# Values of two attention units multiplied in one block, and a new order of the split work in the projections

## The reference, cut to what matters

```python
h = _layernorm(x, axis=-1) * (1 + ca) + sa
Q = X @ W_q.T;  K = X @ W_k.T;  V = X @ W_v.T          # 16 heads of 16 features
Qr = _rope(Qh, cos, sin);  Kr = _rope(Kh, cos, sin)
scores = jnp.einsum('bhqd,bhkd->bhqk', Qr, Kr) * DH ** (-0.5)
scores = jnp.where(causal[None, None], neg, scores)
pattern = jax.nn.softmax(scores, axis=-1)
heads = jnp.einsum('bhqk,bhkd->bhqd', pattern, Vh)
```

## Time and profile before

| | |
|---|---|
| median of 3 runs | 2427.26 us (2424.31 to 2429.4) |
| profiled execution, its time | 2421.51 us |
| profiled execution, its span | 2419.7 us |
| PE busy over the span | 2186.0 us (90%) |
| DVE busy | 1670.5 us (69%) |
| ACT busy | 1299.3 us (54%) |
| mean granted PE clock | 0.949 of full |
| projections, from the span's start to the first products of attention | some 176 us |
| the stages of attention | 215.1 to about 1082 us |
| everything behind attention | some 1338 us |

### The profile page before, as it was taken

The page is one execution under the profiler, slowest core; times in us unless marked ns, Lnnn a source line. Parts: engine busy times, 40 slices in busy tenths (PEclk is TensorE's granted clock), DMA queues, the critical chain, the costliest instruction groups (busy, mean ns, idle before and its releaser), DMA issues. The chain is left out here.

```text
span 2419.7 us, 38970 instructions
## 1 busy us (share of the span) xinstructions
PE 2186.0 (90%) x12976; PEld 1396.1 (58%) x12976; DVE 1670.5 (69%) x2718; ACT 1299.3 (54%) x2506; POOL 878.8 (36%) x1060
## 2 busy tenths in 40 slices
PE   7878999999999999988999599963999999999991
PEld 6752333333333333326777456643888898888891
DVE  7758787878778787815777778874555655555566
ACT  4533777777677777773332344421555555555553
POOL 4552330313121220212555422454345444445351
PEclk9986999999999999999999899985999999999996
DMA  5669025436161611003000100113544434444426
GB/s 199 147 161 124 1 77 110 84 86 115 55 130 57 124 72 46 1 16 121 1 0 0 34 1 1 36 44 125 182 146 142 145 136 140 162 170 142 138 75 222
DMA packets 127399, 227.92 MB, mean 94 GB/s; under 512 B 16689, under 2 KB 91057, under 8 KB 126833
## 3 DMA queue, kind: packets, MB, share of 16 engines
q1 hardware_dynamic: 112672, 180.95, 22.2%
q0 software_dynamic: 14544, 44.61, 11.0%
HBM read 146.65 MB, written 78.48 MB: 93 GB/s over the span
## 5 line engine op out<-in xcount | busy, mean ns | idle before, releaser
L232 DVE TENSOR_REDUCE tile_max<-p_m 128x2 f32<-128x1024 f32 (+1 forms) x628 | 641.9, 1065 | 133.8 <-PE p_m L224 66.7
L1021 ACT ACTIVATE probs<-p_s 128x512 f32<-128x512 f32 (+3 forms) x1280 | 596.4, 534 | 238.5 <-PE p_s L924 233.3
L2302 PE MATMUL p_up<-f_xT,f_w 128*128 128x512 f32 (+1 forms) x2304 | 464.5, 351 | 12.8 <-issue 5.9
L2302 PEld LDWEIGHTS p_up<-f_xT,f_w 128*128 128x128 f32 x2304 | 368.3, 189 | 66.4 <-issue 16.3
L864 POOL TENSOR_SCALAR_AFFINE_SELECT probs<-probs 128x128 f32<-128x128 f32 x512 | 145.3, 293 | 694.0 <-ACT probs L1021 685.2
L221 PE MATMUL p_m<-ka,qa 96*128 96x512 bf16 (+1 forms) x1256 | 352.3, 363 | 12.7 <-DVE tile_max L232 5.0
L924 PE MATMUL p_s<-qa,ka 99*128 99x512 bf16 (+3 forms) x1280 | 351.3, 351 | 13.1 <-ACT probs L1021 7.1
L2471 POOL TENSOR_TENSOR f_w<-f_raw,f_w 128x1024 fp32r<-128x1024 f32 x95 | 231.8, 2450 | 357.1 <-ACT f_w L2357 357.1
L938 PE MATMUL p_o<-probs,va 128*32 128x512 f32 (+3 forms) x2560 | 300.2, 541 | 0.8 <-issue 0.5
L2317 PE MATMUL p_y<-f_w,f_hidden 128*128 128x256 f32 x1872 | 251.1, 280 | 1.0 <-DVE f_hidden L2424 0.6
L221 PEld LDWEIGHTS p_m<-ka,qa 96*128 96x128 bf16 x1256 | 108.3, 99 | 237.7 <-DVE tile_max L232 135.7
(11 more groups left out here) (285 smaller groups left out, 2640.1 us busy)
## 6 DMA issues: line engine op xcount, KB each, us to landing
x_slots<-mods SPq DMA_DIRECT2D x73, 516.0 KB, 4.0
f_raw<-in_W SPq DMA_DIRECT2D x24, 1024.0 KB, 10.9
f_raw<-in_W1a SPq DMA_DIRECT2D x23, 1024.0 KB, 6.0
f_raw<-in_W1b SPq DMA_DIRECT2D x23, 1024.0 KB, 8.3
qk_scr<-parts SPq DMA_DIRECT2D x48, 256.0 KB, 2.8
qa<-qk_scr POOLq DMA_DIRECT2D x42, 256.0 KB, 15.6
ka<-qk_scr POOLq DMA_DIRECT2D x42, 256.0 KB, 17.4
g_ys<-y_rows SPq DMA_DIRECT2D x16, 512.0 KB, 8.8
```

The source lines that it names most:

```text
L232: return nc.vector.tensor_reduce(out=k.tile_max[:, 2 * hp:2 * hp + 2, i, bank], in_=products[:, :, 0:width], op=ALU.max, axis=AX.X)
L1021: nc.scalar.activation(probs[:, (buf * UNITS + n) % NPROBS, h, lo:CH], p_s[:, s_bank(("exp", HG * n + h), buf), lo:CH], ACT.Exp, scale=DH ...
L2302: last = nc.tensor.matmul(p_up[:, f % 2, ab, 0:size], w1[:, wh, ab * KT + kt, f * P:(f + 1) * P], xT[:, t % 2, xh, kt, 0:size], start=(kt, ...
```

## The change

In attention, the values of units n-2 and n-1 are multiplied together at the end of every even unit n, behind both groups of products for the maxima. The buffers for probabilities grow from three to four. In the projections ACT centers the next chunk first and rounds the next chunk's `hT` behind the first part of Q; DVE subtracts Q's first part before it takes K's first half, and makes the rest of `hT` behind that.

```diff
@@ projections, DVE
+                    split(i, 0)
+                    rotate(i, 1, range(1))
                     rest_of_hT(i + 1, 1 - par)
-                    rotate(i, 1, range(1))
-                    split(i, 0)
                     rotate(i, 1, range(1, 2))
@@ projections, ACT
                 def chunk(i, par):
-                    if not first(i):
-                        split_first(i - 1, 1)
                     if not last_chunk(i):
                         center(i + 1)
                     if not first(i):
+                        split_first(i - 1, 1)
                         split_second(i - 1, 1)
                     if not last_chunk(i):
-                        round_hT(i + 1, 1 - par)
                         take_v(i)
                     split_first(i, 0)
+                    if not last_chunk(i):
+                        round_hT(i + 1, 1 - par)
                     split_second(i, 0)
@@ attention
-        NPROBS, NSCORES = 3, 3
+        NPROBS, NSCORES = 4, 3
@@ attention, PE, stage
                         for pair in range(2):
                             scores(s, buf, n, 2 * pair, more)
                             scores(s, buf, n, 2 * pair + 1, more)
-                            if pair:
-
-                                if n:
-                                    values(s, buf, n - 1)
-                                elif not first(s):
-                                    values(s - 1, (buf - 1) % NBUF, UNITS - 1)
                             for u in maxima_of(n, pair, more):
...
+                        if n % 2 == 0:
+
+                            for back in (2, 1):
+                                if n:
+                                    values(s, buf, n - back)
+                                elif not first(s):
+                                    values(s - 1, (buf - 1) % NBUF, UNITS - back)
@@ attention, PE, after the last stage
-                values(NS - 1, (NS - 1) % NBUF, UNITS - 1)
+                for back in (2, 1):
+                    values(NS - 1, (NS - 1) % NBUF, UNITS - back)
```

## The result

The kernel after takes 2474.31 us in the median (2469.86 to 2480.55, four runs), the one before 2425.78 (2423.98 to 2429.4). The ratio is 1.0202, with a 95% interval of 1.0184 to 1.0221: 48.5 us slower. The forecast was 2468, slower.

A forecast was written before the change was run, and what follows sets the result against it. PE, busy 90% of the span, was taken as the bound, setting attention's pace. Attention +50 (7 x 6.5 + 5) and projections -9 on 2421.5 gave 2462.5, plus 5.8 to the median: 2468 us; range 2445 to 2488, over all cases 2425 to 2490.

The forecast's parts named there:

- The bound of before: In inner attention stages PE sets the pace, busy 107.08 of 108.18 us; DVE has 20 us of slack.
- What merging saves: In attention, one entry and exit of 32-column matmuls less per second unit: 0.19 us, 20 times a stage, 3.8 (1.7 to 4.7).
- the walk: Hand timing of an inner attention stage over 20 unit pairs: windows 79.8 plus value blocks 34.9, 114.7 us against 108.2.
- +6.5 a stage by new waits: In inner attention stages, 10.1 us of new waits overrun the 3.6 saved, making each stage 6.5 us longer.
- The signs: Trace marks foretold: stages of 113 to 117 us, PE busy under 106, DVE idle behind blocks, attention starting at about 206.
- The reductions as the cause: In attention, DVE holds at most 2.28 us of reductions against a 3.5 us gap, so PE waits for them afterwards.
- The rival that the saving comes through: In attention, DVE's 20 us slack a stage absorbs the bursts: -30 and -9, total 2388 us; chance 0.09.
- The rival of half the stalls: In attention, waits come to 5 instead of 10 us a stage: +11 with -9, total 2429 us; chance 0.15.
- The floor by ACT: In attention, three score buffers wait for exponentials, so a pair can't end before 3.2 us; two products lose 0.6.
- The last stage, +5: In attention's last stage, the part with products adds 2.5 us and about eight pairs without add 0.3 each: +5.
- The projections, -9: Four chunks with statistics save 2.1 us each, two without 0.5 each; -9, bounds -4 (transfers behind) and -10.
- The sum: Whole kernel: 2421.5 + 50 - 9 = 2462.5 us for the profiled execution, 5.8 more for the median, 2468.

The follow-up runs named there:

- e5: The kernel before with reductions of the maxima cut to the last 128 columns of each half: 2404.71 us, ratio 0.9912.
- e7: The kernel before with short reductions and exponentials of 128 queries per score, other probabilities set to 1: 2396.97 us, ratio 0.9889.
- e8: After's attention with before's projections, short reductions and short exponentials as in e7: 2379.81 us, ratio 0.9818, 17.2 us faster than e7.
- e6: After's attention with before's projections and short reductions as in e5: 2401.79 us, ratio 0.9903.
- e9: The kernel after with the first group of products moved ahead of the first two scores in odd units: 2500.73 us, ratio 1.0311.
- e2: After's projections with before's attention: 2420.63 us, ratio 0.9978 to the kernel before.
- e10: e2 with the store of the next chunk's values issued on SP ahead of the first stage's loads: 2420.12 us, ratio 0.9981.

## Why the prediction was right, point by point

- **The bound of before.** PE set the pace of an inner stage and hardly waited for DVE: taking 47 us of DVE's work a stage away (87.67 to 40.35) gains 0.8 us (e5). Right.
- **What merging saves: 0.19 a block, 3.6 to 3.8 a stage.** Laid bare in the seventh stages of e7 and e8: 3.4 us, or 0.17 a block. Right within its bounds, a little below the 3.6 that the walk used. In the trace of after a block of two full units takes 1.85 to 1.86 us, where two single ones take 2.0.
- **+6.5 a stage by new waits.** Measured +7.2. The walk holds pair by pair, within 0.25 us in 19 of the 20 pairs of the third stage. Its windows for (5,6), (27,28) and (31,32) were 5.7, 3.2 and 6.0 us up to the block, which with the block of 2.0 makes 7.7, 5.2 and 8.0. The trace of after has them from unit to unit in three stretches:

```profile
454.86:462.63 7.77, 6.83 (x48) 2.46 (x44) 6.35 (x7) 5.17 (x10) 0.00 (x0) 1.00 0.14 56
518.49:523.71 5.22, 5.22 (x41) 2.22 (x37) 2.52 (x4) 4.03 (x8) 0.00 (x0) 1.00 0.00 0
530.14:538.08 7.94, 6.80 (x48) 2.43 (x45) 5.83 (x9) 4.66 (x9) 0.00 (x0) 1.00 0.15 58
```

  The worst miss is pair (19,20), 7.08 us where the walk gives 6.4. These 0.7 us are all of the difference between 6.5 and 7.2. The turned rows of maxima take one of the three score buffers there, and the next two scores wait for the exponentials of unit 19, where the walk priced the rows at PE's time alone (0.32):

```profile
498.34 0.39 PE L947 MATMUL p_s<-identb,max_parts 128*12 128x128 bf16 x4
498.88 0.88 PE L924 MATMUL p_s<-qa,ka 99*128 99x512 bf16 x2 [0.16 <-ACT probs L1023]
```
- **The signs.** A stage of 113 to 117 us, 16 value matmuls in 1.9 us, DVE idle behind each block and periods of 15.8 us were all seen. Two signs were not. PE busy for less than 106 us a stage was 108.34: the forecast left out what a wait hides in the busy column. Attention's first unit at about 206 came at 210.3.
- **The reductions as the cause.** Shown by e6: with them short the loss of 54 us turns into a gain of 3.6. The rival that the saving comes through fell: DVE's average slack of 20 us did not absorb the bursts. That two buffers are the reason follows from the walk; no run gives DVE a third. The rival of half the stalls fell too, with 7.2 us more a stage in place of 1.4.
- **The floor by ACT.** The walk had it, but too low. With short reductions it gave 103.2 a stage and 106.9 was measured; with the exponentials short too, the seventh stage falls from 106.3 to 103.1. In the whole forecast this was hidden, probably because where DVE makes PE wait, ACT catches up. It mattered as soon as the experiments took DVE away, and it made e9's sign wrong.
- **The last stage, +5.** Measured +5.8 (106.13 against 100.28). The timeline of PE in its units without products shows the pair of 5.27 us that was forecast as 5.25:

```profile
1114.73 0.82 PE L924 MATMUL p_s<-qa,ka 99*128 99x512 bf16 x3
1115.87 2.35 PE L924 MATMUL p_s<-qa,ka 99*128 99x512 bf16 x5 [0.32 <-ACT probs L1023]
1118.14 1.92 PE L938 MATMUL p_o<-probs,va 128*32 128x512 f32 x16
1120.00 0.82 PE L924 MATMUL p_s<-qa,ka 99*128 99x512 bf16 x3
```

- **The projections, -9.** Measured -4.8 in the trace, and -4.4 in e2's time. The period of a chunk with statistics was forecast as 15.8 and is 15.78 to 15.85 in three of the four. The term that was most mis-sized is the sixth period, forecast as about 15.2 and measured as 17.25: the late stores, of which the prediction said that they would give "the lower one" of its bounds, -4. That is 2.0 of the missing 4 us or so. Another 0.8 is the first chunk with statistics (16.59), and 0.5 the first period, which stays at 15.7. The last 1.0 is no loss that can be put down to the change: the first product starts at 21.09 us in after and at 20.07 before, and it scatters from 20.1 to 21.4 over the traces, with either order above 20.8 at times. The lower bound was the better value. Taking one store forward (e10) doesn't mend it.
- **The sum.** +54.5 for +50, -4.8 for -9, and 1.4 behind attention for 0: 51 in the trace where 41 was forecast, 48.5 between the medians. That 2468 lies only 6 us from the measured 2474 is in part luck: the forecast added 5.8 us from the profiled execution to the median, where the kernel after needs 1.8 (2472.5 to 2474.3). Execution against execution it was 10 us too low.

## What to carry to other kernels

A block of matmuls that feeds nobody is also a gap in the feed of every other engine. Before merging two such blocks, compare the gap with the work that the buffers hold (here 3.5 us against 2.3), not with the consumer's average slack. Where an order is written out by hand, the work between two uses of a buffer is what hides the wait for it; moving that work and leaving the rest of the list as it is undoes the list. And where two consumers with few buffers hang on one producer, a cure for one has to be walked through for the other too.

## What the runs showed that I had not expected

- The two halves of the edit are not additive: the place alone costs 38 us of attention's time, the doubling alone 41, both 54.5.
- In e8, where PE runs ahead of its old pace, it meets the transfer of the maxima's rows in the second stage (2.38 us) and loses clock behind that wait. A stop of 1.3 us that the profile calls only "issue" stands inside a block of the third stage, and no run here says what it is.
- In the trace of after, a DVE operation of 128x4 values in the statistics takes 1.14 and one 2.12 us, and both end within 0.2 us of a POOL operation that runs beside them. The new order leaves this as it was, and no run here separates it:

```profile
96.80 2.39 POOL L358 TENSOR_TENSOR rem<-rot 128x1024 f32<-128x1024 f32 x1 [3.56 <-DVE rot L434]
99.15 2.16 POOL L364 TENSOR_TENSOR parts<-rem,parts 128x1024 bf16<-128x1024 f32 x1
```

```profile
98.07 1.14 DVE L144 TENSOR_TENSOR mean<-stats 128x4 f32<-128x4 f32 x1
...
99.21 2.12 DVE L146 TENSOR_TENSOR ve<-stats 128x4 f32<-128x4 f32 x1
```
